# Output products of an attention kernel taken one head per step over the next group, with a PSUM bank of their own

## The chip, the cores and the metric

The kernel runs on one core of a Trainium2 chip. The metric is device microseconds of one execution. The kernel before takes 1042.69 us, the median of three runs (1040.18 to 1048.0).

## The reference

The input x has 32 sequences of 32 tokens with 512 values. A first layer adds to x a product with a 32 by 32 matrix that each sequence picks by an index. The second layer is attention over a paged cache, cut here to what matters:

```python
q = rope(rmsnorm(x @ Wq.T), pos)          # 32 query heads of 128
k, v = rope(rmsnorm(x @ Wk.T), pos), x @ Wv.T   # 8 key heads
k_all = concat([k_cache[block_table], k])  # 16 pages of 32 old keys, then 32 new keys
v_all = concat([v_cache[block_table], v])
scores = where(valid, q @ k_all.T * SCALE, -1e30)   # old keys count up to cache_seqlens
o = softmax(scores) @ v_all
return x + einsum('bse,de->bsd', o, Wo)    # o has 32 heads x 128 = 4096 values per token
```

Everything is float32. The kernel keeps that precision by writing each float16 operand of a product as a high and a low part and adding three products: high by high, high by low, low by high.

## The kernel before, in words

The first third (to about 370 us) computes the first layer and the projections, and writes queries, key pages and value pages to DRAM in the split form. The rest is a loop of 256 **steps**, one for each sequence (batch b, 32 of them) and key head j (8). A step has 128 rows, four query heads by 32 tokens, against 544 keys. Four batches, so 32 steps, are a **group**: their 128 tokens make one tile of the output. Each engine runs its own list of work over the step number i, and semaphores order them:

- TensorE in step i: `transpose_p(i)` turns the probabilities of step i into a bank of `ps_t` (four f32 transposes), unless the DMA does it; every fourth step `transpose_new` does the same for the 32 new keys of four steps; `scores(i + 3)` (six products, the second half after the row maximum of the step before has left the shared bank); `weigh(i - 2)` (12 products into `ps_o`); every fourth step `weigh_new`; then the output products, if the step has any.
- VectorE in step i: `masked_max(i + 3)` (mask, scale and row maximum), `row_recip(i + 2)`, the low parts of what leaves PSUM: `ot_lo` (every fourth step), `tn_lo` (the new keys' transpose, every fourth step), `t_lo(i)`. A wait in this list holds all that is behind it.
- ScalarE: the high parts of the same (`ot_hi`, `tn_hi`, `t_hi`), then `exp(i + 3)`. GpSimd: scaling of the probabilities by the reciprocal (`norm`) and the loads of value rows (`load_v`), four for a batch.
- SyncE's queue: the loads of queries (`load_queries`), of the 16 key pages of a batch (`load_pages`, by page number, in slots after steps 5, 6, 7 and 0 of a batch), of new values, residuals and stores, and the DMA transposes (`turn_rows(i)`, issued in step i - 2 after `rows_lo` has made the low part of its rows). Keys are held for two batches: the load of batch b + 2 starts in step 5 of batch b and has to be there in step 5 of batch b + 1, when `scores` of batch b + 2 start.

`by_dma(i)` says which steps the DMA transposes: from the second group on steps 2 to 11 of a group (8 to 11 in the second), 64 in all. These are the steps that also carry the output.

The **output products** of a group (`project_out`) are 32 heads by three products of 128 x 512. Before, they run in steps 2 to 9 of the next group, four heads in a step, in two halves of 16 heads. Each half is summed in a bank of `ps_o` that weighing has free for four steps, and `add_residual` adds it to the residual. The transposes have three banks (`NTB = 3`), `ps_s` three and `ps_o` two, which makes eight. The context `ot_hi`, `ot_lo` is stored head by head, batch by batch, token by token; the weights of one head's products are 128 neighbouring values.

The page's lines: the output products are on L1411 (`products`, a helper that phase 1 uses too) with tiles `ps_o<-wo,ot_hi` and `ot_lo`; L1489 is `weigh`, L1503 `weigh_new`, L1449 and L1453 `scores`, L1460 and L1468 the transposes, L1154 the row maximum, L1186 `ot_lo`, L963 `ot_hi`, L1179 `tn_lo`, L1169 `rows_lo`, L1196 the sum with the residual, L627 the query load, L640 a key page, L754 a DMA transpose.

## Time and profile before

| | |
|---|---|
| median of three runs | 1042.69 us |
| the profiled execution | 1046.1 us, span 1044.3 us |
| TensorE busy (8329 products) | 982.7 us, 94% of the span |
| VectorE, ScalarE, GpSimd busy | 795.1, 717.4, 493.7 us |
| granted TensorE clock, mean | 0.993 of 2.4 GHz |
| chain that ended last | TensorE 54%, VectorE 16%, SyncE's queue 8%, DMA 7%, issue 6% |
| DMA | 296.49 MB, 284 GB/s; SyncE's queue holds 71.3% of the 16 engines' span, GpSimd's 19.3% |

The span runs from the first to the last instruction; the time also has what lies around it, 1.8 us here. Products are pipelined and their ends are modelled, so prices are read from one start to the next. A share of busy time is an average over stretches with different limits.

### The profile page before, as it was taken

How to read it: one execution, taken by the hardware profiler on the slowest of the kernel's cores; microseconds unless marked ns; L12 is line 12 of the kernel's file. 1: busy time of each engine (PE TensorE's matmuls, PEld its weight loads, DVE VectorE, ACT ScalarE, POOL GpSimd, SP SyncE). 2: the span in 40 equal slices, each digit the busy share in tenths (PEclk: the TensorE clock that was granted, in tenths of full speed). 3: DMA queues.
4: the chain of work that ended last, by engine and by line, in shares of the span. 5: the costliest groups of instructions: out<-in, count | busy, mean ns of one | idle time of the engine just before them, and what ended most of it. 6: DMA issues, size and time to landing. Idle time of an engine off the chain costs nothing.

```text
span 1044.3 us, 24950 instructions
## 1 busy us (share of the span) xinstructions
PE 982.7 (94%) x8329; PEld 779.9 (75%) x8329; DVE 795.1 (76%) x1705; ACT 717.4 (69%) x1959; POOL 493.7 (47%) x642
## 2 busy tenths in 40 slices
PE   4889999999889999899999999998999999999998
PEld 2678888887678788769768857965976986895793
DVE  6779999999997788758847856865784885786680
ACT  4898999988765778747746746754774774675670
POOL 5445665566881266516415523622441641552340
PEclk9999999999999999999999999999999999999999
DMA  5789999989989899778998998999899999899740
GB/s 202 247 278 336 322 390 367 385 279 398 380 288 326 309 337 343 266 192 294 323 235 267 357 234 243 328 241 228 301 291 243 294 329 241 260 354 249 240 148 11
DMA packets 268016, 296.49 MB, mean 284 GB/s; under 512 B 94064, under 2 KB 225648, under 8 KB 265328
## 3 DMA queue, kind: packets, MB, share of 16 engines
q1 hardware_dynamic: 249200, 227.65, 71.3%
q0 software_dynamic: 18688, 67.25, 19.3%
q8 instruction: 67, 1.10, 0.4%
q14 instruction: 61, 0.50, 0.1%
HBM read 231.77 MB, written 46.27 MB: 266 GB/s over the span
## 4 chain that ended last, share of the span: by engine, by line
PE 54%; DVE 16%; SPq 8%; DMA 7%; issue 6%; ACT 5%; POOL 2%; ACTq 0%; DVEq 0%; POOLq 0%
PE ps_o L1411 16%; PE ps_proj L1411 15%; PE ps_o L1489 8%; SPq L640 5%; PE ps_s L1449 4%; PE ps_s L1453 4%; PE ps_t L1460 3%; DVE probs L1154 2%; DMA vs<-v_pages,v_row 2%; DMA kt<-k_pages_t 2%; PE ps_rt L1559 2%; DVE rot L1282 2%; DVE c_stage L1310 2%; PE ps_o L1503 1%; ACT probs L930 1%
## 5 line engine op out<-in xcount | busy, mean ns | idle before, releaser
L865 POOL TENSOR_SCALAR probs<-probs,recip 128x544 f32<-128x544 f32 (+1 forms) x256 | 157.5, 615 | 382.2 <-DVE recip L1162 377.7
L930 ACT ACTIVATE probs<-probs,neg_max 128x544 f32<-128x544 f32 x256 | 191.3, 747 | 155.5 <-DVE neg_max L1154 154.7
L1154 DVE CUSTOM_DVE_ANT_0 probs<-ps_s,mask,row_scale 128x544 f32<-128x544 f32 x256 | 200.1, 782 | 126.3 <-PE ps_s L1453 123.5
L1489 PE MATMUL ps_o<-pt,vs 128*128 128x128 f16 x3072 | 214.3, 220 | 8.2 <-DMA pt<-wo 3.8
L1489 PEld LDWEIGHTS ps_o<-pt,vs 128*128 128x128 f16 x3072 | 192.3, 98 | 19.0 <-issue 6.6
L821 POOL TENSOR_TENSOR roped<-rot 128x256 f32<-128x256 f32 x160 | 144.2, 922 | 82.2 <-DVE rot L1274 76.3
L1411 PE MATMUL ps_proj<-wt_hi,x0t_hi 128*128 128x512 f32 x384 | 159.7, 416 | 8.0 <-DVE x0t_lo L1112 7.0
L1411 PE MATMUL ps_o<-wo,ot_hi 128*128 128x512 f16 x512 | 153.7, 382 | 10.4 <-DVE ot_lo L1186 10.4
L1411 PE MATMUL ps_proj<-wt_hi,x0t_lo 128*128 128x512 f32 x384 | 151.7, 395 | 0.0
L1411 PE MATMUL ps_proj<-wt_lo,x0t_hi 128*128 128x512 f32 x384 | 150.8, 393 | 0.0
L853 POOL DMA_INDIRECT vs<-v_pages,v_row x128 | 131.4, 1026 | 22.3 <-issue 20.2
L1449 PE MATMUL ps_s<-kt,qt 128*128 128x256 f16 (+1 forms) x768 | 136.4, 287 | 1.9 <-DMA kt<-k_pages_t 1.7
L1174 DVE SCALAR_TENSOR_TENSOR pt<-ps_t,pt 128x512 f16<-128x512 f32 x192 | 130.7, 681 | 4.8 <-ACT pt L937 2.7
L1453 PE MATMUL ps_s<-kt,qt 128*128 128x288 f16 (+1 forms) x768 | 126.2, 273 | 6.7 <-DVE neg_max L1154 6.5
L1460 PE MATMUL ps_t<-fixed,probs 128*128 128x128 f32 x768 | 117.6, 276 | 2.3 <-POOL probs L865 1.1
L937 ACT ACTIVATE pt<-ps_t 128x512 f16<-128x512 f32 x192 | 111.2, 579 | 5.3 <-PE ps_t L1460 5.3
L998 ACT ACTIVATE squares<-ps_proj 128x128 bf16<-128x128 f32 x320 | 85.1, 296 | 21.7 <-PE ps_proj L1411 21.6
L1411 PE MATMUL ps_o<-wo,ot_lo 128*128 128x512 f16 x256 | 97.6, 381 | 0.0
L1453 PEld LDWEIGHTS ps_s<-kt,qt 128*128 128x128 f16 x768 | 73.4, 98 | 27.5 <-DVE neg_max L1154 12.9
L1411 PEld LDWEIGHTS ps_o<-wo,ot_hi 128*128 128x128 f16 x512 | 47.7, 98 | 59.5 <-DVE ot_lo L1186 9.8
L1411 PEld LDWEIGHTS ps_proj<-wt_hi,x0t_hi 128*128 128x128 f32 x384 | 72.9, 190 | 25.2 <-DVE x0t_lo L1112 11.8
L1449 PEld LDWEIGHTS ps_s<-kt,qt 128*128 128x128 f16 x768 | 74.2, 98 | 22.0 <-DMA kt<-k_pages_t 3.2
(146 smaller groups left out, 1599.0 us busy)
## 6 DMA issues: line engine op xcount, KB each, us to landing
kt<-k_pages_t SPq DMA_DIRECT2D x512, 128.0 KB
c_nat<-in_L_cond_k_cache SPq DMA_DIRECT2D x32, 512.0 KB, 5.8
q_t<-stage SPq DMA_DIRECT2D x64, 256.0 KB, 7.3
c_nat<-in_L_cond_v_cache SPq DMA_DIRECT2D x32, 512.0 KB, 7.2
qt<-q_t SPq DMA_DIRECT2D x32, 512.0 KB, 6.2
w_nat<-in_L_cond_Wq SPq DMA_DIRECT2D x8, 1024.0 KB, 8.9
k_pages_t<-c_stage SPq DMA_DIRECT2D x16, 512.0 KB, 5.8
c_nat<-in_L_cond_Wo SPq DMA_DIRECT2D x16, 512.0 KB, 7.7
```

The source lines that it names most:

```text
L821: last = pool.tensor_tensor(dst, a, b, ALU.add)
L853: pool.indirect_dma_start(vs[b % 2][:, c].rearrange("p j s d -> p (j s d)"), None, v_pages, bass.IndirectOffsetOnAxis(ap=v_row[:, b * NCH ...
L865: pool.tensor_scalar(part, part, col(recip, i), 1.0, ALU.mult, ALU.mult).then_inc(p_norm, 1)
L930: act.activation(pr, pr, ACT.Exp, bias=col(neg_max, i), scale=-1.0, accum_out=col(row_sum, i)).then_inc(a_exp, 1)
L937: act.activation(pt_part(i, 0), ps_t[tjob_no["t", i] % NTB][:], ACT.Copy, scale=P_SCALE).then_inc(a_thi, 1)
L1154: dve.tensor_tensor_reduce(out=probs_of(i), in0=ps_s[:, score_cols(i):score_cols(i) + KEYS], in1=mask[(i // HK) % 2][:, mask_at(i):mask_at ...
L1174: dve.scalar_tensor_tensor(pt_part(i, 1), ps_t[tjob_no["t", i] % NTB][:], P_SCALE, pt_part(i, 0), ALU.mult, ALU.subtract).then_inc(v_tlo, 1)
L1411: ins = pe.matmul(ps, a, b, start=first and n == 0, stop=last and n == len(pairs) - 1)
L1449: pe.matmul(own[0], q[:, a], k[:, b, own[1]:own[2]], start=n2 == 0, stop=n2 == 2)
L1453: ins = pe.matmul(shared[0], q[:, a], k[:, b, shared[1]:shared[2]], start=n2 == 0, stop=n2 == 2)
L1460: ins = pe.transpose(ps_t[tjob_no["t", i] % NTB][:, c * P:(c + 1) * P], probs_of(i)[:, SEQ * (i % 2) + c * P:SEQ * (i % 2) + (c + 1) * P], ...
L1489: ins = pe.matmul(ps_o[n % 2][:, jl * P:(jl + 1) * P], v[:, part, :], pt[i % NPT][:, NCH * half + c, :], start=jl == 0 and c == 0 and k == ...
```

## The change

- Each group's output is computed over nearly the whole next group: in its step -1 (the last of the group itself) the first head, then one head a step, two in steps 3 and 4, the last in step 28. For the last group 4, 6, 6 and 16 heads follow in steps -1 to 2. One sum over all 32 heads stands in a bank `ps_y` of its own, and `add_residual` runs once for a group, in step 29.
- The bank comes from the transposes, which have two from step 28 on. Before that `ps_y` serves them as the third.
- `ot_hi` and `ot_lo` stay single. So that the next group can write where heads are already done, their order changes from group to group: in odd groups the head is the innermost index (stride of a head's values 32), in even groups eight heads are (stride 8), tokens in the order token, batch. The copies out of `ps_o` therefore read it with a step and write runs of 16 or 8. Residual loads and stores follow the token order of the group. `t_y` counts quarters of the heads, and `ot_hi` of batch a of the next group waits for quarter a.
- The DMA transposes every fourth step (i % 4 == 3) from step 39 on, 55 in all.
- The 16 key pages are spread over six slots: 3, 2, 3, 3, 3, 2 after steps 5, 6, 7, 0, 1 and 2. DMA transposes are issued in steps 1 and 5, ahead of that step's pages. The store of a group and the load of a residual move from the third to the second batch of a group, one group later.

The diff without the lines that only replace the bank's name in `t_hi`, `tn_hi`, `t_lo` and `tn_lo`:

```diff
@@ -212 @@
     ptn = [sb(f"ptn{i}", [4 * SEQ, 2, P], F16) for i in range(2)]
-    ot_hi = sb("ot_hi", [P, HQ, GB, SEQ], F16)
-    ot_lo = sb("ot_lo", [P, HQ, GB, SEQ], F16)
+    QUARTER = HQ // GB
+    ot_hi = sb("ot_hi", [P, HQ * GB * SEQ], F16)
+    ot_lo = sb("ot_lo", [P, HQ * GB * SEQ], F16)
     result = [sb(f"result{i}", [P, HID]) for i in range(2)]
     ps_s = psum("ps_s", [P, 3 * CH])
-    NTB = 3
+    NTB = 2
     ps_t = [psum(f"ps_t{i}", [P, CH]) for i in range(NTB)]
     ps_o = [psum(f"ps_o{i}", [P, HPC * P]) for i in range(2)]
+    ps_y = psum("ps_y", [P, HID])
     phase2.close()
@@ -419 @@
     AHEAD, BEHIND = 3, 2
-    STEPS = NP2 + 2 * HPC + 3
+    STEPS = NP2 + HPC
     GSTEPS = GB * HK
-    YPARTS = 8
-    YHEADS = HQ // YPARTS
-    YWIN = YPARTS // NHALF
     NBG = GB * NHALF
@@ -432 @@
     TN, TNE, OE = HPC - 1, HPC, HPC + 2
-    DMA_FIRST, DMA_LAST, STAGED = 2, 11, 3
+    DMA_FIRST, STAGED, T_THIRD = 39, 3, 28
     def by_dma(i):
-        g, r = divmod(i, GSTEPS)
-        return 0 < i < NP2 and g >= 1 and (DMA_FIRST if g > 1 else 8) <= r <= DMA_LAST
+        return DMA_FIRST <= i < NP2 and i % HPC == HPC - 1
@@ -474 @@
     tjob_no = {t: n for n, t in enumerate(tjobs)}
-    def y_part(i):
-        g, k = divmod(i - (GSTEPS + 2), GSTEPS)
-        return (g, k) if 0 <= g < NG and k < YPARTS else None
+    t_banks = [0]
+    for kind, i in tjobs[1:]:
+        t_banks.append((t_banks[-1] + 1) % (3 if (i if kind == "t" else HPC * i + TN) < T_THIRD else NTB))
+    def t_bank(kind, i):
+        return (*ps_t, ps_y)[t_banks[tjob_no[kind, i]]]
+    def held_by(n):
+        return max((m for m in range(n) if t_banks[m] == t_banks[n]), default=-1)
+    Y_AT = {r: (r + 1,) for r in range(-1, 3)} | {3: (4, 5), 4: (6, 7)} | {r: (r + 3,) for r in range(5, HQ - 3)}
+    Y_LAST = {-1: range(0, 4), 0: range(4, 10), 1: range(10, 16), 2: range(16, HQ)}
+    Y_OUT, Y_OUT_LAST = HQ - 3, 3
+    def y_group(i):
+        return (i + 1) // GSTEPS - 1
+    def y_heads(i):
+        g = y_group(i)
+        return (Y_AT if g + 1 < NG else Y_LAST).get(i - GSTEPS * (g + 1), ()) if g >= 0 else ()
     def y_out(i):
-        g, k = divmod(i - (GSTEPS + 2 + YWIN), GSTEPS)
-        return NHALF * g + k // YWIN if 0 <= g < NG and k in (0, YWIN) else None
-    def ps_y(w):
-        return ps_o[(w + 1) % 2]
+        g = y_group(i)
+        return g if g >= 0 and i - GSTEPS * (g + 1) == (Y_OUT if g + 1 < NG else Y_OUT_LAST) else None
+    def head_at(g, n):
+        if g % 2 == 1:
+            return n
+        k, j = divmod(n, QUARTER)
+        return HQ // NHALF * (k // NHALF) + NHALF * j + k % NHALF
+    def head_tokens(tile, g, n):
+        if g % 2 == 1:
+            return tile[:].rearrange("p (m h) -> p m h", h=HQ)[:, :, n]
+        k, j = divmod(n, QUARTER)
+        return tile[:].rearrange("p (k m j) -> p k m j", k=GB, j=QUARTER)[:, k, :, j]
+    def row_order(rows, g):
+        return rows if g % 2 == 1 else rows.rearrange("(a t) h -> t a h", a=GB)
@@ -544 @@
         b, h = divmod(n, NHALF)
-        hh = HQ // NHALF
-        return tile[:, hh * h:hh * (h + 1), b % GB, :]
+        g, a = divmod(b, GB)
+        if g % 2 == 1:
+            return tile[:].rearrange("p (a t s h) -> p a s t h", a=GB, t=SEQ, s=NHALF)[:, a, h]
+        return tile[:].rearrange("p (s q a j) -> p s q a j", s=NHALF, a=GB, j=QUARTER)[:, h, :, a]
@@ -556 @@
             eng.wait_ge(v_tnlo, i + 1)
+    def context(n):
+        return ps_o[n % 2][:].rearrange("p (h t) -> p t h", t=SEQ if n // NBG % 2 == 1 else NHALF * SEQ)
@@ -736 @@
                     sp.wait_ge(d_out[g % 2], 16 * (g // 2))
-                sp.dma_start(result[g % 2][:], x0_d[g]).then_inc(d_res[g % 2], 16)
+                sp.dma_start(result[g % 2][:], row_order(x0_d[g], g)).then_inc(d_res[g % 2], 16)
             def store_out(g):
-                sp.wait_ge(v_res, NHALF * (g + 1))
-                sp.dma_start(out[GB * g:GB * (g + 1)].rearrange("b s t -> (b s) t"), result[g % 2][:]
+                sp.wait_ge(v_res, g + 1)
+                sp.dma_start(row_order(out[GB * g:GB * (g + 1)].rearrange("b s t -> (b s) t"), g), result[g % 2][:]
                              ).then_inc(d_out[g % 2], 16)
@@ -754 @@
-            PAGES_IN = {5: 0, 6: 4, 7: 8, 0: 12}
+            PAGES_IN = {5: (0, 3), 6: (3, 2), 7: (5, 3), 0: (8, 3), 1: (11, 3), 2: (14, 2)}
             for i in range(NP2):
@@ -763 @@
                         load_queries(n)
-                    load_pages(n, PAGES_IN[r], NPP // len(PAGES_IN))
+                    load_pages(n, *PAGES_IN[r])
                 if r == 2 and 1 <= b < B - 1:
                     load_new_v(b + 1)
                     for k in WO_WITH_KEYS.get(b, ()):
                         load_wo(k)
                 g, a = divmod(b, GB)
-                if r == 3 and a == 2:
-                    if g >= 1:
-                        store_out(g - 1)
-                    load_residual(g)
+                if r == 3 and a == 1 and g >= 1:
+                    if g >= 2:
+                        store_out(g - 2)
+                    load_residual(g - 1)
+            load_residual(NG - 1)
+            store_out(NG - 2)
             store_out(NG - 1)
@@ -950 @@
...
             def ot_hi_of(n):
                 act.wait_ge(t_pvn, n + 1)
                 if n == 0:
                     all_stored(act)
-                g, first = divmod(n, NBG)
-                if first < NHALF and g >= 1:
-                    act.wait_ge(t_y, NHALF * (g - 1) + first + 1)
-                act.activation(ot_of(ot_hi, n), ps_o[n % 2][:].rearrange("p (h t) -> p h t", t=SEQ), ACT.Copy,
-                               scale=1.0 / P_SCALE).then_inc(a_othi, 1)
+                g, a = divmod(n // NHALF, GB)
+                if g >= 1:
+                    act.wait_ge(t_y, GB * (g - 1) + a + 1)
+                act.activation(ot_of(ot_hi, n), context(n), ACT.Copy, scale=1.0 / P_SCALE).then_inc(a_othi, 1)
@@ -1171 @@
...
             def ot_lo_of(n):
                 dve.wait_ge(a_othi, n + 1)
-                dve.scalar_tensor_tensor(ot_of(ot_lo, n), ps_o[n % 2][:].rearrange("p (h t) -> p h t", t=SEQ),
-                                         1.0 / P_SCALE, ot_of(ot_hi, n), ALU.mult, ALU.subtract).then_inc(v_otlo, 1)
-            def add_residual(w):
-                g, half = divmod(w, NHALF)
-                dve.wait_ge(t_y, w + 1)
-                if w >= 1:
-                    dve.wait_ge(v_res, w)
-                if half == 0:
-                    dve.wait_ge(d_res[g % 2], 16 * (g // 2 + 1))
-                dve.scalar_tensor_tensor(result[g % 2][:], ps_y(w)[:], y_unscale[:, 0:1], result[g % 2][:],
+                dve.scalar_tensor_tensor(ot_of(ot_lo, n), context(n), 1.0 / P_SCALE, ot_of(ot_hi, n),
+                                         ALU.mult, ALU.subtract).then_inc(v_otlo, 1)
+            def add_residual(g):
+                dve.wait_ge(t_y, GB * (g + 1))
+                dve.wait_ge(d_res[g % 2], 16 * (g // 2 + 1))
+                dve.scalar_tensor_tensor(result[g % 2][:], ps_y[:], y_unscale[:, 0:1], result[g % 2][:],
                                          ALU.mult, ALU.add).then_inc(v_res, 1)
@@ -1385 @@
                     add_residual(y_out(i))
-                if at(i, OE) is not None and y_part(i) is not None:
-                    ot_lo_of(at(i, OE))
                 if by_dma(i + 2):
                     row_recip(i + 2)
                 if i + AHEAD < NP2:
                     masked_max(i + AHEAD)
                 if i + 2 < NP2 and not by_dma(i + 2):
                     row_recip(i + 2)
-                if at(i, OE) is not None and y_part(i) is None:
+                if at(i, OE) is not None:
                     ot_lo_of(at(i, OE))
@@ -1455 @@
                 pe.wait_ge(p_norm, i + 1)
-                evacuated(pe, tjob_no["t", i] - NTB)
+                evacuated(pe, held_by(tjob_no["t", i]))
                 for c in range(NCH):
-                    ins = pe.transpose(ps_t[tjob_no["t", i] % NTB][:, c * P:(c + 1) * P],
+                    ins = pe.transpose(t_bank("t", i)[:, c * P:(c + 1) * P],
                                        probs_of(i)[:, SEQ * (i % 2) + c * P:SEQ * (i % 2) + (c + 1) * P], ident[:])
                 ins.then_inc(t_t, 1)
             def transpose_new(n):
                 pe.wait_ge(p_norm, HPC * (n + 1))
-                evacuated(pe, tjob_no["tn", n] - NTB)
+                evacuated(pe, held_by(tjob_no["tn", n]))
                 for m in range(2):
-                    ins = pe.transpose(ps_t[tjob_no["tn", n] % NTB][0:2 * SEQ, m * P:(m + 1) * P],
+                    ins = pe.transpose(t_bank("tn", n)[0:2 * SEQ, m * P:(m + 1) * P],
                                        probs[:, (2 * n + m) % (NPR // 2), L:L + 2 * SEQ], ident[:])
@@ -1476 @@
                     pe.wait_ge(v_otlo, n - 1)
-                    g, first = divmod(n, NBG)
-                    if g >= 1 and 1 <= first <= NHALF:
-                        pe.wait_ge(v_res, NHALF * (g - 1) + first)
                 if by_dma(i):
@@ -1505 @@
-            def project_out(g, k):
+            def project_out(g, n):
+                h = head_at(g, n)
                 if g == 0:
-                    wo_done(pe, YHEADS * (k + 1))
-                w, kk = divmod(k, YWIN)
-                w += NHALF * g
-                if kk == 0:
-                    pe.wait_ge(v_otlo, min(NBG * (g + 1) + k // YWIN, NHB))
-                for h in range(YHEADS * k, YHEADS * (k + 1)):
-                    hi, lo = (o[:, h].rearrange("p b t -> p (b t)") for o in (ot_hi, ot_lo))
-                    ins = products(ps_y(w)[:], [(hi, wo[:, h, 0, :]), (hi, wo[:, h, 1, :]), (lo, wo[:, h, 0, :])],
-                                   first=h == YHEADS * YWIN * (k // YWIN), last=h == YHEADS * YWIN * (k // YWIN + 1) - 1)
-                if kk == YWIN - 1:
+                    wo_done(pe, h + 1)
+                if n == 0:
+                    if g == 0:
+                        evacuated(pe, max(m for m in range(len(tjobs)) if t_banks[m] == NTB))
+                    else:
+                        pe.wait_ge(v_res, g)
+                    pe.wait_ge(v_otlo, NBG * (g + 1) - 1)
+                if n == HQ // NHALF:
+                    pe.wait_ge(v_otlo, NBG * (g + 1))
+                hi, lo = head_tokens(ot_hi, g, n), head_tokens(ot_lo, g, n)
+                ins = products(ps_y[:], [(hi, wo[:, h, 0, :]), (hi, wo[:, h, 1, :]), (lo, wo[:, h, 0, :])],
+                               first=n == 0, last=n == HQ - 1)
+                if n % QUARTER == QUARTER - 1:
                     ins.then_inc(t_y, 1)
@@ -1586 @@
                     weigh_new(at(i, HPC - 1 + BEHIND))
-                if y_part(i) is not None:
-                    project_out(*y_part(i))
+                for n in y_heads(i):
+                    project_out(y_group(i), n)
```

## Rows read from the trace of the kernel before

**Rows 1.** Table of windows: stretch, its length, busy per engine, granted clock, DMA share, GB/s
```profile
426.50:1020.15 593.65, 568.99 (x5912) 453.22 (x5911) 418.47 (x1088) 374.16 (x814) 244.67 (x333) 0.99 0.93 265
687.62:777.00 89.38, 83.32 (x840) 66.44 (x841) 59.78 (x157) 53.47 (x116) 34.96 (x48) 0.96 1.02 262
```

**Rows 2.** Waits of TensorE from 426.5 us on: total us, times, longest
```profile
PE ps_o L1411 <- DVE ot_lo L1186: 10.4, 8, 1.9
PE ps_s L1453 <- DVE neg_max L1154: 4.1, 7, 0.6
...
PE ps_o L1489 <- issue: 1.2, 6, 0.2
```

**Rows 3.** Timeline of TensorE, steps without a head: start us, duration, line, operation
```profile
507.75 0.61 PE L1503 MATMUL ps_o<-ptn,vn 128*128 128x128 f16 x8
508.20 0.61 PE L1460 MATMUL ps_t<-fixed,probs 128*128 128x128 f32 x4
508.64 0.57 PE L1449 MATMUL ps_s<-kt,qt 128*128 128x320 f16 x3
...
509.34 0.83 PE L1489 MATMUL ps_o<-pt,vs 128*128 128x128 f16 x12
510.01 0.61 PE L1460 MATMUL ps_t<-fixed,probs 128*128 128x128 f32 x4
510.45 0.38 PE L1468 MATMUL ps_t<-fixed,probs 128*64 128x128 f32 x2
510.67 0.49 PE L1449 MATMUL ps_s<-kt,qt 128*128 128x256 f16 x3
```

**Rows 4.** Timeline of all engines, end of a block of heads and after it
```profile
716.09 0.78 DVE L1154 CUSTOM_DVE_ANT_0 probs<-ps_s,mask,row_scale 128x544 f32<-128x544 f32 x1 [1.67 <-PE ps_s L1453]
...
716.80 0.74 DVE L1169 SCALAR_TENSOR_TENSOR wo<-probs,split_by,wo 128x512 f16<-128x512 f32 x1
...
724.19 0.83 PE L1489 MATMUL ps_o<-pt,vs 128*128 128x128 f16 x12
724.39 0.78 DVE L1154 CUSTOM_DVE_ANT_0 probs<-ps_s,mask,row_scale 128x544 f32<-128x544 f32 x1 [0.94 <-PE ps_s L1453]
...
725.29 0.42 DVE L1179 SCALAR_TENSOR_TENSOR ptn<-ps_t,ptn 64x256 f16<-64x256 f32 x1
725.31 0.49 PE L1449 MATMUL ps_s<-kt,qt 128*128 128x256 f16 x3
...
729.94 1.46 PE L1489 MATMUL ps_o<-pt,vs 128*128 128x128 f16 x12 [3.78 <-DMA pt<-wo]
```

**Rows 5.** Chain of waits in order of time: start us, us, what
```profile
524.05 2.59 PE ps_o L1411 x12
...
583.47 5.92 DMA kt<-k_pages_t
```

**Rows 6.** SyncE's queue: timeline of its issues, and the line of its DMA transposes
```profile
572.26 0.48 SPq L627 DMA_DIRECT2D qt<-q_t  x1
...
573.90 9.91 SPq L640 DMA_DIRECT2D kt<-k_pages_t  x16
...
720.18 1.89 SPq L640 DMA_DIRECT2D kt<-k_pages_t  x4
...
L754 SPq DMA_TRANSPOSE pt<-wo x64: 1232/1262/5369, 454.0 to 975.0; - x64
...
DMA to landing us min/median/max: 2.8/4.0/11.8
```

**Rows 7.** Groups by line: copies out of PSUM, and weight loads (busy us, mean ns)
```profile
L963 ACT ACTIVATE ot_hi<-ps_o 128x512 f16<-128x512 f32 x57 | 33.2, 583 | 34.0 <-PE ps_o L1411 27.8 <-PE ps_o L1503 6.1
L1186 DVE SCALAR_TENSOR_TENSOR ot_lo<-ps_o,ot_hi 128x512 f16<-128x512 f32 x57 | 38.6, 677 | 4.1 <-ACT ot_hi L963 4.1
...
L1411 PEld LDWEIGHTS ps_o<-wo,ot_hi 128*128 128x128 f16 x512 | 47.7, 98 | 59.5 <-DVE ot_lo L1186 9.8 <-issue 3.4
...
L1411 PEld LDWEIGHTS ps_proj<-wt_hi,x0t_hi 128*128 128x128 f32 x240 | 45.2, 188 | 7.9 <-DVE wt_lo L1122 0.6
```

More of the change, by code:

```diff
@@ L936, in t_hi @@
                     act.wait_ge(t_pv, i - NPT + 1)
-                act.activation(pt_part(i, 0), ps_t[tjob_no["t", i] % NTB][:], ACT.Copy, scale=P_SCALE).then_inc(a_thi, 1)
+                act.activation(pt_part(i, 0), t_bank("t", i)[:], ACT.Copy, scale=P_SCALE).then_inc(a_thi, 1)
             def rows_hi(i):
@@ L952, in tn_hi @@
                 act.activation(ptn[n % 2][0:2 * SEQ].rearrange("p m r -> p (m r)"),
-                               ps_t[tjob_no["tn", n] % NTB][0:2 * SEQ, 0:2 * P], ACT.Copy, scale=P_SCALE
+                               t_bank("tn", n)[0:2 * SEQ, 0:2 * P], ACT.Copy, scale=P_SCALE
                                ).then_inc(a_tnhi, 1)
@@ L1173, in t_lo @@
                 dve.wait_ge(a_thi, pe_no(i + 1))
-                dve.scalar_tensor_tensor(pt_part(i, 1), ps_t[tjob_no["t", i] % NTB][:], P_SCALE, pt_part(i, 0),
+                dve.scalar_tensor_tensor(pt_part(i, 1), t_bank("t", i)[:], P_SCALE, pt_part(i, 0),
                                          ALU.mult, ALU.subtract).then_inc(v_tlo, 1)
@@ L1179, in tn_lo @@
                 dve.scalar_tensor_tensor(ptn[n % 2][2 * SEQ:4 * SEQ].rearrange("p m r -> p (m r)"),
-                                         ps_t[tjob_no["tn", n] % NTB][0:2 * SEQ, 0:2 * P], P_SCALE,
+                                         t_bank("tn", n)[0:2 * SEQ, 0:2 * P], P_SCALE,
                                          ptn[n % 2][0:2 * SEQ].rearrange("p m r -> p (m r)"), ALU.mult, ALU.subtract
```

## The prediction, made before the changed kernel was run

> **What bounds the kernel now.** I read first the table of windows, over the attention stretch from 426.5 us to the last block of output products at 1020.15 us: TensorE is busy 568.99 of 593.65 us, so it is the bound, and at most 24.7 us of standing can be won there. Its granted clock is 0.99 over the stretch, about 5 us lost; 0.96 over 89.38 us of one group, 3.6 us, is most of it [rows 1]. In that group TensorE had stood still for 3.78 us behind a DMA transpose, and after it the clock was partly at 1.2 instead of 2.4 GHz [rows 1, 4]. The list of waits names the standing: 10.4 us for ot_lo ahead of the output products (eight times), 4.1 us for the row maximum, 1.2 us of issue gaps, the rest under 4 us a line [rows 2].
>
> The timeline of TensorE gives the prices, from start to start: weighing new keys 0.45 us, the transposes of a step 0.44, scores 0.70, weighing 0.67, the new-key transpose 0.22 [rows 3]. In the chain of waits four heads of the output take 2.59 us, so one takes 0.65, and the last page of a burst of 16 lands 5.92 us after its issue [rows 5].
>
> **What the change removes.** The blocks of four heads per step go, and with them the wait of the first block for ot_lo (y now starts a step after it) and that of weighing for the borrowed bank (y has its own). The steps without any head, in which VectorE has about as much to do as TensorE, shrink from 24 to two of 32. I take out the whole idle time and the whole loss of clock, 24.7 + 5 = 29.7 us, and put back below each wait that I can derive. The output has 768 products in either kernel.
>
> **What it adds.** Transposes by DMA fall from 64 to 55 (one in four from step 39), so TensorE does nine more: 9 x 0.44 = 4.0 us. On ScalarE and VectorE these nine swap the two halves of a split of rows (VectorE 0.74 us) for the two halves of a copy out of PSUM (the form of ot_hi and ot_lo, 0.58 and 0.68 us); GpSimd scales nine full rows more. All of it lies under TensorE: VectorE is busy 418, ScalarE 374, GpSimd 245 of 593.65 us [rows 1, 4, 7].
>
> **The bank that is given away.** With two transpose banks the transposes of step 4n+5 wait until VectorE has emptied the new-key transpose of step 4n+3. It does so in step 4n+4, behind the row maximum and the reciprocal. The rows show that chain: weighing starts at 724.19, the maximum at 724.39, and tn_lo ends at 725.29 + 0.42 = 725.71, which is 1.52 us after weighing starts [rows 4]. In the new step TensorE has weighing and one head until then, 0.67 + 0.65 = 1.32 us. So it waits 0.20 us, in seven of the eight quads of a group (one has two heads in that step) and in seven groups: 49 x 0.20 = 9.8 us. The third bank hides this now. Two steps of group 0 come on top, with two banks already: step 29 without a head, 1.52 - 0.67 = 0.85 us, and step 32, which waits for the copy of step 31 (0.68 us in place of 0.42, no other head): 0.5 us; 1.4 us together. No such wait is in the trace, so bounds: 0, if modelled ends of matmuls hide a fifth of a microsecond; 0.39 us each, 19 us, if the f32 weights of the transpose (0.19 us) are loaded only once the wait is over [rows 7]. I take 0.20, the row of the same chain.
>
> **Steps 29 and 30** of a group have no head. TensorE needs 2 x (0.70 + 0.67 + 0.44) + 0.45 = 4.1 us there; VectorE two maxima with reciprocals (0.90 each, 724.39 to 725.29), rows_lo 0.74, ot_lo, two copies and the group's sum at 0.68 each: 5.3 us [rows 3, 4, 7]. It enters with room, so the wait is between 0 and 1.2 us a group. I take 0.4, as one maximum alone is awaited in the step after: 7 x 0.4 = 3 us.
>
> **SyncE's queue and the key pages.** Take as zero the first scores of a batch, in step 5 of the batch before; the next batch's pages have to be there eight steps later. Four steps cost 4 x (0.70 + 0.67 + 0.65) + 3 x 0.44 + 0.22 + 0.45 = 10.1 us; eight, with two bank waits, 20.5 us. The transpose issued in step 5 waits for rows_lo: scores 0.70, 0.20 to the maximum, 1.45 from there to the end of rows_lo (716.09 to 717.54) [rows 4]: 2.35 us. What is queued behind it is the whole load of the batch. Its issue takes 1.26 us; the first page follows the query load by 1.64 us; a page takes 0.47 us and a slot 0.78 us more ((9.91 - 4 x 1.89) / 3) [rows 6]. The eleven pages of four slots are issued by 2.4 + 1.3 + 1.6 + 11 x 0.47 + 3 x 0.78 = 12.8 us. Then stands the transpose of step 1, ready at 10.3 + 2.35 = 12.7 us, and behind it the last five pages, issued by 12.8 + 1.3 + 2.4 + 1.6 = 18.1 us. That leaves 2.4 us to land. Bounds: 5.92 us in the burst of 16 [rows 5]; at most 3.24 us for four pages behind a transpose, the last issued at 722.07 and its scores running without a wait at 725.31 [rows 4, 6]; below, no wait at all. I take 2.5 us, from the second row, as it has the new pattern: 28 batches x 0.1 = 2.8 us.
>
> A transpose itself is needed 10.3 + 0.7 - 2.4 = 8.6 us after issue, and lands after 4.0 us in the median, 11.8 at the longest [rows 6]: nothing. If that cover goes, it costs what the 3.78 us above cost. The stores and residual loads, moved on this queue, are awaited two dozen steps later: nothing.
>
> **Emptying ps_o** now reads PSUM with a step and writes runs of 8 or 16 elements. The rows have 0.58 and 0.68 us for long runs and nothing like the new order [rows 7]. Below: no change; above: doubled, which would delay the first head of a group by up to 1.2 us, 8 us in all. I take no change, since both are one element after the other of the same count.
>
> **The tail.** Of the last block's wait I leave 0.7 us, as half of the heads no longer stand behind it, and the 1.2 us of issue gaps stay [rows 2].
>
> **The sum.** The profiled execution took 1046.1 us (span 1044.3), 3.4 above the median of 1042.7. 1046.1 - 29.7 + 4.0 + 9.8 + 1.4 + 3 + 2.8 + 0.7 + 1.2 = 1039.3, so 1039 us, 0.3% under the median: most of what the blocks cost comes back as waits at a bank.
>
> **Rivals.** *Packed* (0.28, faster): the chain through the row maximum is no longer than TensorE's 1.32 us, pages land in time, and steps 29 and 30 are covered: 1039 - 9.8 - 2.8 - 3 = 1023 us. For it: a fifth of a microsecond hangs on modelled ends. Against: the starts of three rows in a row [rows 4].
>
> *Late pages* (0.17, slower): the five pages behind the transpose of step 1 land later than 2.4 us after issue, and from there each 0.1 us costs 2.8 us: 1039 - 2.8 + 28 x 0.84 = 1060 us at the bound of 3.24, 1135 us at the 5.92 of a burst. For it: the DMA engines' share is 0.93 over the stretch [rows 1], and two transposes a batch now sit in the queue of every load. Against: the pause that the transpose makes lets the eleven pages before it drain.
>
> *Strided weights* (0.05, slower): the 128 columns of a head's weights now lie 16 or 64 bytes apart, before side by side. A load takes 98 ns now and 188 ns at the slowest (f32); both hide under a product of 0.22 us [rows 7]. Past that the load sets the pace: at twice the f32 one, 768 x (0.38 - 0.22) = 123 us, 1162 us.
>
> The Trainium skill (Advanced Engine Details and Errata, SBUF Cachelines) speaks for this rival: lines have 16 bytes, and going to another line with each access costs a penalty, which here would be every column. It also says (TensorE: Matmul & The Clock Gate, Weight-path perf modes) that a fast weight load reads chunks "packed or strided". No run so far shows such a load. By the first rule the time would be the rival's, by the second the sum's.
>
> **How the numbers follow.** Forecast 0.50, packed 0.28, late pages 0.17, strided 0.05. The forecast's own range is 1031 to 1052: bank waits from 0.05 to 0.39 us, 0 to 1.2 us for steps 29 and 30, ps_o up to 8 us. The range of 1023 to 1061 takes in half of packed and late pages to the bound of 3.24; some 0.2 stay out. A measurement here cannot tell less than 1% from no change: 1032 to 1053. Packed and a little of the forecast give faster 0.29, most of the forecast and the mildest late pages same 0.50, the rest slower 0.21.
>
> **What would show it.** Right: waits of the transposes into ps_t for VectorE's emptying of the new keys, near 49 times 0.2 us; none for result, hardly any for ot_lo; 201 x 4 transposes; clock at 1.00. Late pages: the first scores of nearly every batch wait for kt. Strided: loads of the heads' weights well over 98 ns. Wrong altogether: under 10 us of idle TensorE in the stretch, or a large wait that none of these names.

## The result, and the profile after

The changed kernel takes 1147.26 us, the median of four runs (1147.05 to 1149.69), against 1045.35 us for the four runs of the kernel before beside it. One of those four, at 1067.97 us, fell in a slower state of the chip and is left out of the comparison; against the other three (median 1042.69 us) the ratio is 1.100, with a 95% interval of 1.094 to 1.105. Forecast were 1039 us and a range up to 1061. It went the way of the rival *late pages*.

The waits of TensorE from 426.5 us on answer [rows 2] (total us, times, longest):

```profile
PE ps_s L1481 <- DMA kt<-k_pages_t: 73.7, 26, 5.0
PE ps_t L1492 <- DVE ptn L1217: 8.6, 49, 0.2
PE ps_t L1500 <- DVE pt L1212: 2.5, 3, 1.1
PE ps_t L1492 <- DVE pt L1212: 0.3, 1, 0.3
```

The waits for `ot_lo` and for the result are gone, and the bank wait is there, 49 times 0.2 us. But the scores wait 26 times, in nearly every batch, for their key pages, 2.8 us each. The table of windows [rows 1] (stretch, length, busy per engine, granted clock, DMA share, GB/s) shows a second loss:

```profile
510.00:600.00 90.00, 79.70 (x788) 66.08 (x787) 53.72 (x142) 48.91 (x108) 34.75 (x46) 0.96 0.85 243
600.00:700.00 100.00, 85.83 (x803) 69.89 (x801) 55.06 (x145) 51.96 (x112) 34.34 (x46) 0.90 0.79 220
...
800.00:900.00 100.00, 85.48 (x830) 70.72 (x828) 56.65 (x150) 53.67 (x116) 35.23 (x48) 0.93 0.77 224
```

Up to 1100 us the granted clock is 0.90 to 0.97 in place of 0.99, and the DMA engines are less busy than before, 0.77 to 0.85. So neither TensorE nor the DMA engines are busy all the time: two things wait for each other in turn. TensorE's timeline at one such wait (start us, duration, line, operation) shows where the clock goes:

```profile
743.41 0.50 PE L1481 MATMUL ps_s<-kt,qt 128*128 128x256 f16 x3 [3.43 <-DMA kt<-k_pages_t]
743.75 0.53 PE L1485 MATMUL ps_s<-kt,qt 128*128 128x288 f16 x3
744.12 1.36 PE L1518 MATMUL ps_o<-pt,vs 128*128 128x128 f16 x12
745.28 1.06 PE L1532 MATMUL ps_o<-ptn,vn 128*128 128x128 f16 x8
746.13 1.06 PE L1443 MATMUL ps_y<-wo,ot_hi 128*128 128x512 f16 x2
...
747.41 0.72 PE L1492 MATMUL ps_t<-fixed,probs 128*128 128x128 f32 x4
747.97 0.57 PE L1481 MATMUL ps_s<-kt,qt 128*128 128x320 f16 x3
```

After standing for 3.43 us, weighing takes 1.16 us from start to start where it had 0.67, the new keys 0.85 for 0.45, a head 1.28 for 0.65: the lower of the two clock levels, for about 3 us (granted clock 0.50 from 745 to 747 us), as after the stand of 3.78 us in [rows 4]. The same work takes some 1.6 us longer. A stretch at the lower level begins in or right after 17 of the 26 waits; the other nine, one of 3.49 us among them, have none.

SyncE's queue in the load before that wait answers [rows 6] (start us, us, line, issue, count); the rows of GpSimd's value loads in the same stretch stand below it:

```profile
721.72 1.30 SPq L791 DMA_TRANSPOSE pt<-wo  x1
723.06 0.57 SPq L664 DMA_DIRECT2D qt<-q_t  x1
...
725.20 8.23 SPq L677 DMA_DIRECT2D kt<-k_pages_t  x11
733.53 1.25 SPq L791 DMA_TRANSPOSE pt<-wo  x1
735.95 2.90 SPq L677 DMA_DIRECT2D kt<-k_pages_t  x5
```

```profile
734.10 1.02 POOL L892 DMA_INDIRECT vs<-v_pages,v_row  x1 [0.15 <-issue]
...
736.35 1.00 POOL L892 DMA_INDIRECT vs<-v_pages,v_row  x1 [0.16 <-issue]
...
739.45 1.02 POOL L892 DMA_INDIRECT vs<-v_pages,v_row  x1 [0.16 <-issue]
...
740.97 1.01 POOL L892 DMA_INDIRECT vs<-v_pages,v_row  x1 [0.17 <-issue]
```

The first scores of the batch before started at 719.33. The last five pages are out at 738.85, 19.5 us later, and there at 743.4, 4.5 us after that: a period of 24.1 us where 20.5 were to be had. The four value loads of the batch go out from 734.10 to 741.98, around the issue and the landing of these five pages. For every batch from 5 to 29 (a load has landed with the last update of its semaphore) the medians are: last page issued 20.2 us after the first scores, landed 4.5 us later, period 24.9. The chain of waits [rows 5] over the whole run now reads

```profile
PE 35%; SPq 26%; DVE 14%; DMA 13%; issue 8%; ACT 3%; POOL 1%; ACTq 0%; DVEq 0%; POOLq 0%
```

with TensorE at 54% and SyncE's queue at 8% before. Of the groups of [rows 7], the copies out of `ps_o` are what they were, and the heads' weight loads are slower, with no wait behind them:

```profile
L1443 PEld LDWEIGHTS ps_y<-wo,ot_hi 128*128 128x128 f16 x512 | 57.2, 148 | 6.2
...
L1224 DVE SCALAR_TENSOR_TENSOR ot_lo<-ps_o,ot_hi 128x512 f16<-128x512 f32 x57 | 38.3, 672 | 8.5 <-ACT ot_hi L1002 8.5
...
L1002 ACT ACTIVATE ot_hi<-ps_o 128x512 f16<-128x512 f32 x57 | 33.2, 582 | 14.3 <-PE ps_o L1532 14.0
```

### The profile page after: what moved, and what is told of

It is laid out like the page before. It is cut to its first block, busy times and chain, and to the rows that moved or that the text cites. A ratio compares the mean times of both kernels' runs of the same rounds, so it can differ in the third digit from the quotient of the medians.

```text
span 1145.5 us, 25083 instructions
## 1 busy us (share of the span) xinstructions
PE 1020.9 (89%) x8365; PEld 832.8 (73%) x8365; DVE 784.3 (68%) x1688; ACT 723.5 (63%) x1959; POOL 496.5 (43%) x642
## 4 chain that ended last, share of the span: by engine, by line
PE 35%; SPq 26%; DVE 14%; DMA 13%; issue 8%; ACT 3%; POOL 1%; ACTq 0%; DVEq 0%; POOLq 0%
PE ps_proj L1443 13%; SPq L677 12%; DMA kt<-k_pages_t 11%; SPq L672 7%; PE ps_y L1443 5%; SPq L791 4%; PE ps_o L1518 4%; PE ps_s L1481 3%; PE ps_s L1485 3%; PE ps_t L1492 2%; DVE probs L1192 2%; PE ps_rt L1592 2%; DVE rot L1316 2%; DVE c_stage L1344 2%; PE ps_o L1532 1%
## 5 line engine op out<-in xcount | busy, mean ns | idle before, releaser
L904 POOL TENSOR_SCALAR probs<-probs,recip 128x544 f32<-128x544 f32 (+1 forms) x256 | 161.1, 629 | 481.6 <-DVE recip L1200 480.3
L1518 PE MATMUL ps_o<-pt,vs 128*128 128x128 f16 x3072 | 223.2, 225 | 0.0
L1518 PEld LDWEIGHTS ps_o<-pt,vs 128*128 128x128 f16 x3072 | 201.8, 101 | 8.2
L1481 PE MATMUL ps_s<-kt,qt 128*128 128x256 f16 (+1 forms) x768 | 140.4, 293 | 74.1 <-DMA kt<-k_pages_t 74.1
L860 POOL TENSOR_TENSOR roped<-rot 128x256 f32<-128x256 f32 x160 | 144.2, 922 | 80.8 <-DVE rot L1308 72.4
L1443 PE MATMUL ps_y<-wo,ot_hi 128*128 128x512 f16 x512 | 157.7, 390 | 0.0
L1481 PEld LDWEIGHTS ps_s<-kt,qt 128*128 128x128 f16 x768 | 74.0, 100 | 91.0 <-DMA kt<-k_pages_t 80.5
L1212 DVE SCALAR_TENSOR_TENSOR pt<-ps_t,pt 128x512 f16<-128x512 f32 x192 | 131.3, 684 | 2.8 <-ACT pt L976 0.8
L1485 PE MATMUL ps_s<-kt,qt 128*128 128x288 f16 (+1 forms) x768 | 130.9, 281 | 2.6 <-DVE neg_max L1192 2.5
L1492 PEld LDWEIGHTS ps_t<-fixed,probs 128*128 128x128 f32 x768 | 92.6, 145 | 53.9 <-issue 38.0
L1492 PE MATMUL ps_t<-fixed,probs 128*128 128x128 f32 x768 | 120.3, 280 | 12.9 <-DVE ptn L1217 9.5
L1443 PE MATMUL ps_y<-wo,ot_lo 128*128 128x512 f16 x256 | 98.8, 386 | 0.0
L1485 PEld LDWEIGHTS ps_s<-kt,qt 128*128 128x128 f16 x768 | 76.1, 101 | 22.7 <-DVE neg_max L1192 5.4
L1443 PEld LDWEIGHTS ps_proj<-wt_hi,x0t_hi 128*128 128x128 f32 x384 | 72.5, 189 | 24.9 <-DVE x0t_lo L1150 11.4
```

What stands on the lines that cost most here:

```text
L860: last = pool.tensor_tensor(dst, a, b, ALU.add)
L904: pool.tensor_scalar(part, part, col(recip, i), 1.0, ALU.mult, ALU.mult).then_inc(p_norm, 1)
L1212: dve.scalar_tensor_tensor(pt_part(i, 1), t_bank("t", i)[:], P_SCALE, pt_part(i, 0), ALU.mult, ALU.subtract).then_inc(v_tlo, 1)
L1443: ins = pe.matmul(ps, a, b, start=first and n == 0, stop=last and n == len(pairs) - 1)
L1481: pe.matmul(own[0], q[:, a], k[:, b, own[1]:own[2]], start=n2 == 0, stop=n2 == 2)
L1485: ins = pe.matmul(shared[0], q[:, a], k[:, b, shared[1]:shared[2]], start=n2 == 0, stop=n2 == 2)
```

## The experiments

Ten kernels were run, each beside the kernel before (median 1041.2 to 1043.5 us). All times are medians; "period" is the median from first scores to first scores of a batch.

| kernel | us | ratio to before, 95% interval | largest waits of TensorE |
|---|---|---|---|
| the change | 1147.3 | 1.094 to 1.105 | key pages 73.7 us |
| e1 four slots | 1062.7 | 1.013 to 1.026 | DMA transposes 12.9, bank 8.7, key pages 2.1 |
| e2 queue part only | 1200.0 | 1.147 to 1.161 | key pages 82.0, DMA transposes 36.9 |
| e3 heads part only | 1196.6 | 1.133 to 1.152 | DMA transposes 72.4, banks 39.5 |
| e4 e1, other phase | 1093.6 | 1.044 to 1.053 | bank 64.3 |
| e5 e4, new keys later | 1034.3 | 0.989 to 0.995 | bank 4.4 |
| e6 numbers by four | 1160.1 | 1.105 to 1.121 | key pages 75.4 |
| e7 no values | 1053.3 | 1.008 to 1.014 | key pages 10.6, bank 8.6 |
| e8 values later | 1168.1 | 1.108 to 1.128 | values 89.2 |
| e9 numbers aligned | 1092.4 | 1.040 to 1.054 | key pages 33.1, bank 8.6 |
| e10 e8 and e9 | 1193.9 | 1.135 to 1.151 | values 103.5 |

**e1, four slots.** The slots of the pages are undone: all sixteen go ahead of the transpose of step 1. With that the queue also has four loads of page numbers in a batch in place of six, so two things change at once; e9 below parts them.

```diff
-            PAGES_IN = {5: (0, 3), 6: (3, 2), 7: (5, 3), 0: (8, 3), 1: (11, 3), 2: (14, 2)}
+            PAGES_IN = {5: (0, 4), 6: (4, 4), 7: (8, 4), 0: (12, 4)}
```

> The changed kernel with one thing undone: the sixteen key pages of a batch are issued in four slots of four again, so that all stand ahead of the transpose of step 1 in SyncE's queue. Theory A, the order of the queue: in the changed kernel the last page is issued 19.5 us after the first scores of the batch before and lands 4.5 us later, 24.0 us against a need at 20.5. With four slots the last page goes out at about 15.3 us and lands at about 19.8: the wait of the scores for kt, 73.7 us now, falls under 10 us, the clock is granted in full again, and the kernel takes 1025 to 1060 us. Theory B, the transposes by DMA (two a batch, all through the kernel) slow the landing of whatever is beside them: the landing grows as the slots are packed closer, waits for kt stay over 40 us and the time stays over 1110 us.

Measured: 1062.7 us, the waits for kt down to 2.1 us. The last page goes out at 16.0 us and lands 2.4 us later (medians). So theory A, the queue as the cause, holds, and B falls: as many DMA transposes are in the queue as in the changed kernel. The time is 3 us over what A gave, and a new wait stands in the list: the transpose of step 1 has sixteen pages ahead of it. Weighing waits ten times for a transpose, nine times for this one:

```profile
PE ps_o L1518 <- DMA pt<-wo: 12.9, 10, 4.0
PE ps_t L1492 <- DVE ptn L1217: 8.7, 49, 0.2
PE ps_t L1500 <- DVE pt L1212: 2.5, 3, 1.1
PE ps_s L1481 <- DMA kt<-k_pages_t: 2.1, 3, 0.9
```

**e2, the queue part alone**, in the kernel before:

```diff
-        g, r = divmod(i, GSTEPS)
-        return 0 < i < NP2 and g >= 1 and (DMA_FIRST if g > 1 else 8) <= r <= DMA_LAST
+        return DMA_FIRST <= i < NP2 and i % HPC == HPC - 1
...
-            PAGES_IN = {5: 0, 6: 4, 7: 8, 0: 12}
+            PAGES_IN = {5: (0, 3), 6: (3, 2), 7: (5, 3), 0: (8, 3), 1: (11, 3), 2: (14, 2)}
```

> The kernel before with only the queue part of the change: each fourth step transposed by DMA from step 39, and the key pages in six slots. The output products stay in blocks of four heads in eight steps of a group, in the borrowed bank. Theory A (the queue is the loss): the load of a batch needs about 24 us from first scores to first scores as in the changed kernel; three of four batches of a group have no heads and take some 16 us of TensorE, so each waits 6 to 8 us for kt, 21 batches together 130 to 170 us: 1150 to 1200 us, slower than the changed kernel itself. Theory C (the loss comes from heads, strides or banks): the time stays within 2% of the kernel before, 1025 to 1065 us.

**e3, the heads part alone**, the changed kernel with the old queue:

```diff
-        return DMA_FIRST <= i < NP2 and i % HPC == HPC - 1
+        g, r = divmod(i, GSTEPS)
+        return 0 < i < NP2 and g >= 1 and (DMA_FIRST if g > 1 else 8) <= r <= DMA_LAST
...
-            PAGES_IN = {5: (0, 3), 6: (3, 2), 7: (5, 3), 0: (8, 3), 1: (11, 3), 2: (14, 2)}
+            PAGES_IN = {5: (0, 4), 6: (4, 4), 7: (8, 4), 0: (12, 4)}
```

> The other half: the changed kernel's output products (one head a step, own bank, two transpose banks, strided ot_hi and ot_lo) with the old queue, ten transposes by DMA in a row in steps 2 to 11 of a group and pages in four slots. Theory A: waits for kt under 15 us in all; what is left are the bank waits (0.2 us each) and the steps behind the row of DMA transposes: 1020 to 1045 us. Theory C (heads, strides or banks): over 1100 us.

Measured: 1200.0 and 1196.6 us. Each half alone is slower than both together. e2 came out on theory A's side, at the upper end of its time and with the clock at 0.92 from 426.5 us on. But it waits 82.0 us for kt, where the theory had 130 to 170, and 36.9 us for the DMA's transposes, which the theory did not name. For e3 both theories were wrong: kt costs 6.8 us, and the largest waits are for the DMA's transposes, 72.4 us in 30 waits. SyncE's queue in one run of ten transposes points to the reason:

```profile
666.74 1.27 SPq L792 DMA_TRANSPOSE pt<-wo  x1
668.81 1.91 SPq L678 DMA_DIRECT2D kt<-k_pages_t  x4
670.82 2.01 SPq L792 DMA_TRANSPOSE pt<-wo  x1
673.34 2.09 SPq L678 DMA_DIRECT2D kt<-k_pages_t  x4
675.53 1.26 SPq L792 DMA_TRANSPOSE pt<-wo  x1
677.29 1.91 SPq L678 DMA_DIRECT2D kt<-k_pages_t  x4
679.29 3.16 SPq L792 DMA_TRANSPOSE pt<-wo  x1
```

With four pages between them the transposes go out 4.2 us apart. A step with four heads and no transposes on TensorE took 0.70 + 0.67 + 2.59 = 4.0 us at the least [rows 3, 5], so the blocks of the kernel before gave the queue its time; with one head a step takes 2.0 us. This is read from the rows, and no run tests it alone; nor does one look into the 39.5 us that e3 waits for banks.

**e4 and e5, another phase.** In e1 the queue has a transpose ahead of the queries (step 5) and one behind the pages (step 1). e4 moves the DMA's transposes to steps 0, 4, 8, so that they are issued in steps 2 and 6:

```diff
# e4, on top of e1
-        return DMA_FIRST <= i < NP2 and i % HPC == HPC - 1
+        return DMA_FIRST <= i < NP2 and i % HPC == 0
```

> The changed kernel with the pages in four slots and the transposes by DMA in steps 0, 4, 8 and so on instead of 3, 7, 11. The transposes are then issued in steps 2 and 6, so the load of a batch (queries in step 5) does not start behind one; the last page is to be issued 15.2 us after the first scores of the batch before, and with 4.5 us of landing is there at 19.7. The new-key transpose then shares no bank with the transposes that follow it by two, so the 49 waits of 0.2 us go too, but other waits for a bank may come. Theory A: 1020 to 1035 us, faster than both kernels. Theory B (transposes slow the landing wherever they stand): waits for kt over 40 us, over 1090 us.

Measured: 1093.6 us, and no wait for kt or pt at all. The theory of the queue is right and the time is wrong, since a wait of another kind came, "PE ps_t L1500 <- DVE pt L1212: 64.3, 57, 1.8": the new keys' transposes now follow those of a step at once, in the bank of the step before, which VectorE has not emptied. e5 puts them behind scores and weighing:

```diff
# e5, on top of e4
-                if at(i, TN) is not None:
+                late = by_dma(i + 1)
+                if at(i, TN) is not None and not late:
                     transpose_new(at(i, TN))
...
                     weigh(i - BEHIND)
+                if at(i, TN) is not None and late:
+                    transpose_new(at(i, TN))
```

> The kernel of e4 (pages in four slots, transposes by DMA in steps 0, 4, 8 ...) with one more edit: from step 39 on the transposes of the new keys stand behind the weighing of their step, not ahead of its scores. In e4 TensorE waited there 57 times, 64.3 us in all (1.13 us each), for VectorE to empty the bank of the transposes two back; scores and weighing, 0.70 + 0.67 = 1.37 us, would cover that. Expected if this wait is all that e4 has left: 1093.6 - 64 = 1026 to 1035 us, no wait for kt or pt over 5 us, clock 0.99 or more, faster than both kernels. Rival, the engines of the DMA become the bound (their share was 0.90 at 1093 us, so 0.96 at 1030): waits for kt or pt of 10 us or more come back and the time stays at 1040 to 1060 us. Second rival: the row maximum, which waits for these transposes, comes later by 0.9 us and makes the next scores wait, 55 x 0.5 us: 1055 to 1065 us.

Measured: 1034.3 us, 0.992 of the kernel before (0.989 to 0.995): faster than both kernels. The gain is small, under the 1% that the prediction could not tell from no change, but all four runs (1032.2 to 1035.2 us) lie below the lowest of the seven of the kernel before (1039.5 us). Both rivals of this expectation fall, as its waits from 426.5 us on and one row of its windows show:

```profile
PE ps_t L1500 <- DVE pt L1212: 4.4, 9, 1.1
PE ps_s L1481 <- DMA kt<-k_pages_t: 1.0, 3, 0.6
```

```profile
600.00:800.00 200.00, 198.02 (x2053) 166.10 (x2052) 137.99 (x369) 129.43 (x281) 87.52 (x117) 1.00 1.02 275
```

TensorE is busy for 99% of these 200 us with the clock in full, so little more is to be had there in this form: the change with its queue put right gains 0.8%. The DMA engines' share is 1.02, as it was in one group of the kernel before [rows 1]; that this is their bound is not shown.

**e6 and e9, the page numbers.** Where do 19.5 to 20.2 us of issue come from, when 18.1 were forecast? In the changed kernel's trace SyncE's loads of page numbers into its registers had grown. The line of these loads, before and after (duration min/median/max in ns):

```profile
L635 SPq TENSOR_LOAD <-page_ids x152: 263/303/1090, 224.5 to 989.9; - x152
```

```profile
L672 SPq TENSOR_LOAD <-page_ids x212: 264/670/1122, 223.6 to 1088.8; - x106
```

e6 loads four numbers for each slot, from the slot's first:

```diff
-                at = b * NPP + first
+                at = min(b * NPP + first, B * NPP - 4)
...
+                width = count if b < 2 else 4
...
-                    page_ids[0:1, at:at + count], ...
+                    page_ids[0:1, at:at + width], ...
```

> The changed kernel, with the six uneven page slots and all else as they are; only the load of page numbers into SyncE's registers takes four numbers for each slot (the surplus is not used) in place of three or two. In the trace of the changed kernel four numbers took 0.30 us, three 0.67 and two 0.47, so six slots cost 3.6 us of queue a batch and would cost 1.8. Theory A (the queue's own time sets the period of 24.9 us a batch): the last page is issued 1 to 1.8 us earlier, 28 batches, so 28 to 50 us less: 1097 to 1120 us. Theory D (the landing of the last pages, not their issue, is the limit, because the DMA engines are full then): the pages are issued earlier but land when they did: 1135 to 1150 us.

Measured: 1160.1 us, and the last page issued at 20.6. The edit missed its aim, so the run does not tell the theories apart: the loads became longer, with a median of 867 ns.

```profile
L675 SPq TENSOR_LOAD <-page_ids x212: 266/867/1238, 225.7 to 1098.1; - x106
```

By their place in the list of numbers, those of four that begin at a multiple of four take 0.30 us, all others about 0.87 (1.14 right behind a DMA transpose); three took 0.67 and two 0.47. e9 keeps the slots and, from batch 2 on, loads the numbers in aligned fours:

```diff
...
+                    for q in range(first // 4, (first + count - 1) // 4 + 1):
+                        if (b, q) not in numbers:
+                            at = b * NPP + 4 * q
+                            _, numbers[b, q] = ...(page_ids[0:1, at:at + 4], ...)
...
+                    pages = [numbers[b, k // 4][k % 4] for k in range(first, first + count)]
```

> e6 mended. In e6 loads of four numbers that begin at a multiple of four took 0.30 us and the others 0.87, so its queue gained nothing (4.3 us a batch for numbers, 3.6 in the changed kernel), and it says nothing on the queue's own time. Here the changed kernel loads its numbers in four groups that begin at a multiple of four and keeps them in registers from slot to slot: 1.2 us a batch, 2.4 less. Theory A (issue and landing add up): last page issued about 1.7 us earlier (the rest goes into the wait for the transpose of step 1), landing still 4.5 us, the period falls from 24.9 to about 23.2: 1095 to 1110 us. Theory D alone (the DMA engines set when the last page lands): 1135 to 1150 us.

Measured: 1092.4 us, a little better than theory A had it, and not D. The profiled execution was the fastest of its five, 1082.2 us.

```profile
L677 SPq TENSOR_LOAD <-page_ids x120: 294/306/678, 364.9 to 1022.4; - x120
```

The last page is issued at 17.6 us (20.2 before), still lands 4.5 us later, and the period is 22.4. So issue and landing add up, and 55 of the 105 us that the change lost (1147.3 against 1042.7) hang on 2.4 us of register loads in each batch, the loss of clock in them included (mean clock 0.991 in the profile, 0.966 in the changed kernel). e1, with four loads a batch as well, is 30 us below e9: that much hangs on the order of the queue.

**e7, e8 and e10, the landing.** e7 leaves out the value loads from batch 2 on and weighs older values; e8 puts them into steps 5 to 8:

```diff
# e7
-                if rest in V_SLOTS and 2 <= b + 1 < B:
-                    load_v(b + 1, V_SLOTS.index(rest))
...
-                    pe.wait_ge(d_vs[b % 2], 16 * NCH * (b // 2 + 1))
+                    pe.wait_ge(d_vs[b % 2], 16 * NCH)
# e8
-            V_SLOTS = (0, 1, 2, 3)
+            V_SLOTS = (3, 4, 5, 6)
```

> The changed kernel without the value loads of batches 2 to 31; it weighs the values of batches 0 and 1 instead, so its results are those of other values. The last five key pages were issued in the same steps as the value loads and took 4.5 us (median) to land, 2.4 us in e1 where they are issued earlier. Theory D (they share the DMA engines with the value loads): landing falls to about 2.5 us, 2 us less in each of 28 batches, waits for kt from 74 to under 40 us, about 1080 to 1095 us. Theory E (the landing is long for another reason, the transposes beside them): landing stays at 4 us or more and the time at 1130 us or more.

> The changed kernel with all its work; only GpSimd's four value loads of a batch are issued in steps 5 to 8, not 2 to 5. Without value loads (e7) the last key pages landed 1.7 us after issue and the kernel took 1053 us. If it is the meeting of the two loads in time that made the landing long, most of that comes back with the loads apart: landing 1.7 to 2.5 us, a period of 21.3 to 22 us a batch, 1053 to 1085 us; the values are needed in step 10 and should be there. Rival: the DMA engines have too much to do in all, whenever it is issued; then the values meet the queries and first pages of the next batch, those are late instead (or the values are, in step 10), and the time stays over 1120 us.

Measured in e7: 1053.3 us, better than expected. With the queue's order unchanged the last page goes out at 19.5 us and lands in 1.7 (4.5 with the values beside it); 10.6 us of waits for kt are left. In e8, too, the pages land in 2.4 us and no scores wait for them. So the meeting in time with the value loads is what makes the landing long. The other runs are in line with it: in e1 the last page is out as the first value load begins and lands in 2.4 us, in e5 it is out 2 us later than that load and lands in 3.5, in the changed kernel 3 us later and lands in 4.5 (medians). But 1168.1 us is on the rival's side: the values come late instead. The wait, and the last value load and the weighing of one batch:

```profile
PE ps_o L1518 <- DMA vs<-v_pages,v_row: 89.2, 29, 7.4
...
745.78 1.01 POOL L892 DMA_INDIRECT vs<-v_pages,v_row  x1 [0.16 <-issue]
753.28 1.46 PE L1518 MATMUL ps_o<-pt,vs 128*128 128x128 f16 x12 [3.65 <-DMA vs<-v_pages,v_row]
```

The expectation had the values needed in step 10 and there in time. The trace gives them less: the last load is out at 746.79, weighing could have begun at 749.63, 2.8 us later (the median too, batches 6 to 29), and in e8 that load lands 5.7 us after its issue (median). That lies between e1 (5.3) and e5 (6.4), where there are some 10 us or more between that issue and the need. So e8 sent its values too late, and does not show what its rival says, that the DMA engines have too much to do in all. Whether a place between the two would serve both loads is not tested. The Trainium skill (DMA: Bandwidth & Descriptors, Queues, rings and completion order) says that each engine takes packets in turn from the queues that it has work for. The trace agrees as far as the pages go: they land in 1.7 us alone and in 4.5 beside the values.

e10, e8 and e9 together:

> e8 and e9 together, so with the changed kernel's order of SyncE's queue untouched (the five pages still stand behind the transpose of step 1). If issue and landing add up, the last page is issued at about 18.5 us and lands by 20.5, when it is needed: waits for kt under 10 us and 1035 to 1055 us. If the order of the queue alone decides, over 1080 us.

Measured: 1193.9 us. The pages are there at 21.0 us and no scores wait for them; the values make TensorE wait 103.5 us, with the same 2.8 us between issue and need as in e8. The expectation had looked at the pages alone.

## Why the prediction was wrong

**The step that failed** is "SyncE's queue and the key pages", in two terms of its sum. *Issue*: "the last five pages, issued by ... 18.1 us" was 20.2 in the median. The row used for a slot, 0.78 us, held a number load of 0.30 us; the new slots of two and three numbers cost 0.47 and 0.67, and the one behind the transpose of step 1 0.96 in the load shown. I had counted the slots and taken the price of each from slots of another size. e9 takes that back: 17.6 us. *Landing*: "I take 2.5 us, from the second row, as it has the new pattern" was 4.5. The row that I used had its pages out at 722.07 [rows 6]; the value loads of that batch began after them, as GpSimd's timeline of the kernel before shows, which I had not read:

```profile
722.32 1.01 POOL L853 DMA_INDIRECT vs<-v_pages,v_row  x1 [0.15 <-issue]
```

The 2.5 was also less than the row itself had: by their semaphore these pages landed 3.1 us after issue, and over batches 5 to 29 of the kernel before the median is 4.0. The new place of the last five pages is among the four value loads. e7 shows 1.7 us without them. What I set against the rival, that the pause at the transpose lets the first eleven pages drain, speaks of those pages; the values come after them.

Put into the rival's own sum, issue and landing are 2.1 + 4.5 = 6.6 us behind 18.1, 4.2 more than the 2.4 there were: 1039 - 2.8 + 28 x 4.2 = 1154 us, 7 over the measured 1147. So the mechanism stood in the prediction, with its place and its price; two inputs were too small, and its chance of 0.17 with them.

**The clock** had no term: I took the whole loss out and put none back, though [rows 4] had the pattern. TensorE's missing time divides as follows. The profiled execution took 1147.2 us, 107.9 over the forecast. Waits for kt are 73.7 against 2.8, 70.9 us. TensorE is busy 1020.9 us against 985.5 in e5, which has the same products and four transposes more: 35.4 us at the lower level. Together they are 106.3 of 107.9. This is an account of TensorE's time and not of two causes: the period is issue and landing, and at full clock TensorE would have waited longer for the same page, except where its slower steps hold the queue up. e7 has the same queue at a clock of 0.997, and its last page is out at 19.5 us against 20.2. So the clock can have added up to 0.7 us to a period, 20 us in 28 batches (an estimate from these two rows); no run parts it from what the values' traffic adds.

**What held.** The bank wait: forecast 49 x 0.20 = 9.8 us, measured 49 times, 8.6. The waits of the blocks are gone. The two steps of group 0: 0.85 and 0.5 forecast, 0.84 (at 420.98) and 0.31 (at 429.51) measured. Three waits, 2.5 us in all, of the new keys' transposes for the bank of the step before were not in the sum. Steps 29 and 30: 3 forecast, no such wait in the list. The copies out of `ps_o` with a step: 582 and 672 ns, as taken. The strided weights: 148 ns for 98, under the 0.216 us of a product, and a head is still 0.65 us from start to start. The Trainium skill (Advanced Engine Details and Errata, SBUF Cachelines) has a penalty where each access goes to another line. The trace agrees with a penalty, 148 ns for 98, but it hides behind the product. That rival is out: e5 has the same weights and takes 1034.3 us.

**The second gap** is in what I costed at nothing: a transpose itself, needed 8.6 us after issue. That holds in the changed kernel, whose list has no wait for pt. It does not hold where the pages go first (e1: 12.9 us in ten waits), nor with ten transposes in a row and no long block steps (e3: 72.4 us).

## What to carry to other kernels

A load that is issued piece by piece has a period: the issue of its last piece, behind all that the queue holds ahead of it, plus the landing of that piece in the traffic of its moment. Take both from rows with the same neighbours, and count the small instructions of the queue (here register loads) at the size that they will have. Where two parts of a change move the same cover, try each alone before judging either: here each half costs 14% to 15%, both together 10%, and both with pages in four slots, the transposes in another phase and the new keys later gain 0.8%.

## What was not expected of the hardware

- A load of four numbers into SyncE's registers takes 0.30 us where they begin at a multiple of four, and 0.87 elsewhere; three take 0.67, two 0.47. The Trainium skill (DMA: Bandwidth & Descriptors, Latency and other measured facts) has a floor of about 600 ns for such loads; the aligned four and the two lie below it.
- A head's weights with 16 or 64 bytes from column to column load in 148 ns, side by side in 98 [rows 7].
- Of the 26 waits of TensorE for key pages, 1.3 to 5.0 us long, 17 have a stretch at the lower clock level in or right after them, of 3 us or more. Length alone does not tell which: one of 1.72 us has it and one of 3.49 us has not.
